# Attention scores of two tiles at once on 32-row parts of the array, and the values' product first in its slot

## What is computed

```
x = x + attn(layernorm(x))               # 16 query heads of 16, 4 key/value heads, causal
x = x + cross(layernorm(x), ctx)         # same heads; keys = values = ctx, no mask; then @ Wc.T + bc
x = x + moe(layernorm(x))                # 64 experts, top 6 of 3 of 8 groups, capacity 96, plus a shared expert

scores = q @ k.T / 4                     # 64 x 64 per sequence and head
probs  = softmax(scores)                 # causal part masked in attn
out    = probs @ v
```

## Time and profile before

| | us |
|---|---|
| runs of the kernel | 842.42, 837.95, 840.81; median 840.81 |
| profiled execution, its own time | 842.78 |
| its span, first to last instruction | 841.0 |
| TensorE matmuls busy | 676.1 (80%) |
| VectorE busy | 482.0 (57%) |
| ScalarE busy | 338.5 (40%) |
| GpSimd busy | 378.1 (45%) |
| TensorE's mean granted clock | 0.905 of full speed |

### The profile page before, as it was taken

The page is one execution under the profiler, slowest core; times in us unless marked ns, Lnnn a source line. Parts: engine busy times, 40 slices in busy tenths (PEclk is TensorE's granted clock), DMA queues, the critical chain, the costliest instruction groups (busy, mean ns, idle before and its releaser), DMA issues. The chain is left out here.

```text
span 841.0 us, 16829 instructions
## 1 busy us (share of the span) xinstructions
PE 676.1 (80%) x6353; PEld 482.3 (57%) x6353; DVE 482.0 (57%) x1086; ACT 338.5 (40%) x636; POOL 378.1 (45%) x354
## 2 busy tenths in 40 slices
PE   2699999998988788888745999799999987773083
PEld 1266666676766566665412556477887765553062
DVE  3267776677868777778445999533333332321057
ACT  2477777766767646755121332112222211110000
POOL 5122222125343423431121832847776777776454
PEclk9899999998999989999756999899999999997555
DMA  7234444665532223210018000138999988953298
GB/s 218 27 59 79 79 79 77 99 98 100 100 73 62 47 45 76 48 44 29 5 44 257 2 0 1 42 96 224 239 235 228 231 211 212 225 127 40 24 302 303
DMA packets 125376, 94.30 MB, mean 112 GB/s; under 512 B 73137, under 2 KB 109169, under 8 KB 125297
## 3 DMA queue, kind: packets, MB, share of 16 engines
q1 hardware_dynamic: 96368, 74.57, 35.1%
q0 software_dynamic: 23552, 14.21, 10.2%
q10 hardware_dynamic: 5376, 4.46, 1.7%
HBM read 60.26 MB, written 24.44 MB: 101 GB/s over the span
## 5 line engine op out<-in xcount | busy, mean ns | idle before, releaser
L1229 POOL DMA_INDIRECT sum_d<-nz,tokens x64 | 118.2, 1847 | 46.8 <-issue 14.6
L724 DVE TENSOR_REDUCE mx<-Sc 128x16 f32<-128x1024 f32 x64 | 77.9, 1217 | 37.8 <-PE Sc L401 37.5
L1056 PE MATMUL bank<-xnT,sgu_sb 128*128 128x512 f32 (+1 forms) x192 | 86.9, 601 | 11.8 <-PEq L1588 11.8
L1111 PE MATMUL bank<-xT,wgu_sb 128*88 128x96 f32 x1024 | 95.1, 246 | 0.3 <-ACT xT L1180 0.3
L1279 DVE TENSOR_TENSOR hid<-sil,bank 88x192 f32<-88x192 f32 x64 | 22.4, 350 | 118.2 <-ACT sil L1186 88.6
L1111 PEld LDWEIGHTS bank<-xT,wgu_sb 128*88 128x88 f32 x1024 | 89.4, 157 | 0.6 <-issue 0.5
L600 ACT COPY ET<-ring 128x512 f32<-128x512 f32 x128 | 69.5, 589 | 44.0 <-PE ring L413 41.8
L429 PEld LDWEIGHTS O<-vbd,ET 128*64 128x64 f32 x2048 | 69.2, 142 | 25.9 <-issue 17.3
L413 PE MATMUL ring<-ident,E 128*128 128x128 f32 x512 | 73.8, 290 | 12.5 <-ACT E L639 11.5
L728 DVE TENSOR_TENSOR E<-Sc,mx 128x1024 f32<-128x1024 f32 x64 | 78.4, 1225 | 6.9 <-DVE mx L724 0.5
L401 PE MATMUL Sc<-kbd,qT 64*64 64x256 f32 x1024 | 76.4, 404 | 6.7 <-DMA kbd<-kT 6.7
(11 more groups left out here) (149 smaller groups left out, 1144.1 us busy)
## 6 DMA issues: line engine op xcount, KB each, us to landing
wgu_sb<-in_wgu_dram SPq DMA_DIRECT2D x64, 352.0 KB
wd_sb<-in_wd_dram SPq DMA_DIRECT2D x64, 176.0 KB
sum_d<-zeros SPq DMA_DIRECT2D x16, 524.0 KB, 6.4
y<-sum_d SPq DMA_DIRECT2D x16, 512.0 KB, 8.8
kbd<-kT SPq DMA_DIRECT2D x248, 32.0 KB, 2.1
X<-in_x_dram SPq DMA_DIRECT2D x8, 512.0 KB, 6.4
rows_d<-xhT SPq DMA_DIRECT2D x8, 512.0 KB, 3.0
out_dram<-X ACTq DMA_DIRECT2D x8, 512.0 KB, 5.2
```

The lines of the kernel that those rows point to most:

```text
L724: nc.vector.reduce_max(mx[:, m % 2, :], sc, AX.X).then_inc(s_mx, 1)
L1056: last = nc.tensor.matmul(out[0:m, :], sgu[:, e, k * MS + m0:k * MS + m0 + m], xnT[:, e, TOK * g:TOK * (g + 1)], start=e == 0, stop=e == 1)
L1111: last = nc.tensor.matmul(GP[e % 2][0:MH, CAP * u:CAP * (u + 1)], wgu[:, j, 4 * MH * c + MH * u:4 * MH * c + MH * (u + 1)], xT[:, e % 2, c ...
L1229: pool.indirect_dma_start(w["sums"][e % 2], bass.IndirectOffsetOnAxis(ap=tokens[0:CAP - 1, e:e + 1], axis=0), outs[0:CAP - 1, e % EB, :], ...
```

## The change

Each product of the scores is cut in two: 32 rows (two heads) by 64 queries, with 128 columns. A pair `p` of tiles is computed in one call, into one PSUM tile `Sc` of four banks, bank `r` for the 32 rows `32r`. The mask is 512 columns wide and goes over both tiles of the pair at once. `scores(p)` waits until VectorE has subtracted both tiles of the pair before. It is called in even slots only, two tiles ahead, and comes after `pv` and `out_t`. `pv(m-1)` moves from the slot's end to its beginning. Waits that counted tiles count pairs. The order of the heads in `E` changes with the banks, and `pair_of` with it. VectorE's two instructions have the same elements in another access pattern.

```
@@ pair_of
-    r, c, m = j // 4, j // 2 % 2, j % 2
-    return 4 * c + 2 * r + m
+    r, c = j // 2, j % 2
+    return 4 * c + r
@@ block_keys (SyncE); the same change in ScalarE's xt and queries
-                    sp.wait_ge(s_sc, 4 * (g - 1))
+                    sp.wait_ge(s_sc, 2 * (g - 1))
@@ TensorE
-            def scores(m):
-                g, t = m // GT, m % GT
+            def scores(p):
+                g, t = 2 * p // GT, 2 * p % GT
                 cross = is_cross(g)
                 if t == 0:
                     pe.wait_ge(s_kbd, KDMA * (g + 1))
                     pe.wait_ge(*saved(("XT1" if cross else "Q1", g)))
-                if m >= 2:
-                    pe.wait_ge(s_sub, m - 1)
-                for c in range(2):
-                    if not cross:
-                        for r, b in ((0, 0), (1, 0), (0, 1), (1, 1)):
-                            rows = slice(64 * r, 64 * (r + 1))
-                            nc.tensor.matmul(Sc[m % 2][64 * b:64 * (b + 1), r, 256 * c:256 * (c + 1)],
-                                             ident_bf[rows, rows], mask[rows, :], start=True, stop=False)
-                    for r, b in ((0, 0), (1, 0), (0, 1), (1, 1)):
-                        rows = slice(64 * r, 64 * (r + 1))
-                        at = 128 * t + 64 * b
-                        last = nc.tensor.matmul(Sc[m % 2][64 * b:64 * (b + 1), r, 256 * c:256 * (c + 1)],
-                                                qT[rows, g % 2, c, at:at + 64],
-                                                kbd[g % 2][rows, c, 2 * t + b].rearrange("p h k -> p (h k)"),
-                                                start=cross, stop=True)
+                if p >= 1:
+                    pe.wait_ge(s_sub, 2 * p)
+                if not cross:
+                    for r in range(0, 4, 2):
+                        for k, b in ((0, 0), (1, 0), (0, 1), (1, 1)):
+                            rows = slice(64 * k, 64 * (k + 1))
+                            nc.tensor.matmul(Sc[64 * b:64 * (b + 1), r + k, :], ident_bf[rows, rows], mask[rows, :],
+                                             start=True, stop=False)
+                for n in range(2):
+                    for c in range(2):
+                        for b in range(2):
+                            at = 128 * (t + n) + 64 * b
+                            for r in range(4):
+                                rows = slice(32 * r, 32 * (r + 1))
+                                last = nc.tensor.matmul(
+                                    Sc[64 * b:64 * (b + 1), r, 256 * n + 128 * c:256 * n + 128 * (c + 1)],
+                                    qT[rows, g % 2, c, at:at + 64],
+                                    kbd[g % 2][rows, c, 2 * (t + n) + b, 2 * (r % 2):2 * (r % 2) + 2].rearrange(
+                                        "p h k -> p (h k)"), start=cross, stop=cross or (n == 1 and c == 1),
+                                    tile_position=(32 * r, 64 * b))
                 last.then_inc(s_sc, 1)
@@ TensorE's slots
             for m in range(FIRST, LAST):
-                if 0 <= m + 1 < 2 * NT:
-                    scores(m + 1)
+                if 0 <= m - 1 < 2 * NT:
+                    pv(m - 1)
                 if crossed(m - 2):
                     out_t(m - 2)
+                if m % 2 == 0 and 0 <= m + 2 < 2 * NT:
+                    scores(m // 2 + 1)
                 if 0 <= m < 2 * NT:
                     probs_t(m)
...
-                if 0 <= m - 1 < 2 * NT:
-                    pv(m - 1)
@@ VectorE's shift(m)
-                dve.wait_ge(s_sc, m + 1)
-                sc = Sc[m % 2][:].rearrange("p r (h k) -> p (r h) k", k=S)
+                dve.wait_ge(s_sc, m // 2 + 1)
+                sc = Sc[:, :, 256 * (m % 2):256 * (m % 2 + 1)].rearrange("p r (h k) -> p r h k", k=S)
@@ memory
-        mem["mask"] = sb("mask", [128, HQ * S], BF16)
+        mem["mask"] = sb("mask", [128, HH * S], BF16)
-        mem["Sc"] = [pb(f"Sc{k}", [128, 2, 512]) for k in range(2)]
+        mem["Sc"] = pb("Sc", [128, 4, 512])
```

More of the change, by code:

```diff
@@ L541, in xt @@
                     if v == 0:
-                        act.wait_ge(s_sc, 4 * (g - 1))
+                        act.wait_ge(s_sc, 2 * (g - 1))
                     nc.scalar.activation(qT[:, g % 2, :, cols].rearrange("p c (t q) -> p c t q", t=2), src,
@@ L721, in shift @@
             def shift(m):
-                dve.wait_ge(s_sc, m + 1)
-                sc = Sc[m % 2][:].rearrange("p r (h k) -> p (r h) k", k=S)
-                nc.vector.reduce_max(mx[:, m % 2, :], sc, AX.X).then_inc(s_mx, 1)
+                dve.wait_ge(s_sc, m // 2 + 1)
+                sc = Sc[:, :, 256 * (m % 2):256 * (m % 2 + 1)].rearrange("p r (h k) -> p r h k", k=S)
+                nc.vector.reduce_max(mx[:, m % 2, :].rearrange("p (r h) -> p r h", r=4), sc, AX.X).then_inc(s_mx, 1)
                 if m >= 2:
@@ L727, in shift @@
                 dve.wait_ge(s_mx, m + 1)
-                nc.vector.tensor_tensor(E_[:, m % 2, :].rearrange("p (h k) -> p h k", k=S), sc,
-                                        mx[:, m % 2, :].unsqueeze(2).to_broadcast([128, H, S]),
+                nc.vector.tensor_tensor(E_[:, m % 2, :].rearrange("p (r h k) -> p r h k", r=4, k=S), sc,
+                                        mx[:, m % 2, :].rearrange("p (r h) -> p r h", r=4).unsqueeze(3).to_broadcast(
+                                            [128, 4, 4, S]),
                                         ALU.subtract).then_inc(s_sub, 1)
@@ L1526, in _ @@
                     nc.gpsimd.affine_select(out=m, in_=m, compare_op=ALU.is_ge, fill=MASKED,
-                                            base=0, pattern=[[0, HQ], [-1, S]],
+                                            base=0, pattern=[[0, HH], [-1, S]],
                                             channel_multiplier=1).then_inc(s_const, 1)
```

## The result

The changed kernel takes 893.36 us (median of 4 runs, 888.49 to 897.22) where the kernel before, timed beside it, takes 839.45 (837.95 to 842.42): 1.0635 times as long, with a 95% interval of 1.0571 to 1.0698. The forecast was 870 with a range of 842 to 892: the sign was right and the size too small, by 23 us, just outside the range. The profiled run took 897.22 us, its span 895.5, its mean granted clock 0.878 (0.905 before).

The account below looks back on a forecast made before the run. TensorE was taken to bound self attention; in cross attention TensorE and VectorE wait for each other. Terms 5 + 10 + 1 + 7 - 6 = +17, plus 12 for the clock, gave +29: 870 us, range 842 to 892.

Parts of the forecast that it names:

- The products' length: Scores in both attentions: eight array parts at once, a cross pair 1.05 us instead of 2.1, self 1.65 instead of 2.42.
- The values' product first: `pv` at the slot's head: cross attention's wait for it goes, 4.0 us a group; self attention's start gains 1.
- The keys a slot later: Self attention: TensorE stands 1.7 us a group for key DMAs, groups take 21.35 us against 20.74; +5 in all.
- The passage: From self to cross attention: key loops of 22.4 and 24.4 us in place of 19.7 and 17.4; +10.
- Until routing: Stretch between the passage to cross attention and the start of routing: +1 us.
- The lone PSUM tile: Cross attention: VectorE stands 2.85 us each even slot, less the vanished `pv` wait; net +7 us over four groups.
- The end: Last three attention slots have no scores and `pv` comes first: -6 us (-2 to -9).
- The clock: Pauses before cross pairs' scores: some ten more falls to half clock at 1.2 us each, +12 (0 to +25).
- the keys' loop of the self groups: Self attention: scores, next key copy, then 13.2 us to landing; 21.35 us against 20.74, +0.6 six times.
- no further falls: Rival for the attentions: the clock falls no more often than before; +17, 858 us, chance 0.24.
- four parts at once: Rival for the scores' products: only four array parts work together; +20, 890 us, chance 0.14.
- hidden transfers: Rival for self attention: key DMAs stay hidden and TensorE remains the bound; 825 us, chance 0.13.

Follow-up runs that it names:

- e6: Changed kernel with the values' product moved back to the slot's end: 995.18 us, 1.1817 times the kernel before.
- e1: Kernel before with only the values' product and `out_t` moved ahead of the scores, to the slot's head: 896.25 us, 1.0667 times the kernel before.
- e8: Changed kernel with half of each group's key transfers (8 of 16) issued from GpSimd's queue instead of SyncE's: 862.85 us, 1.0264 times the kernel before.
- e4: Changed kernel with ten idle products filling TensorE's pause before the pair's scores: 871.33 us, 1.0359 times the kernel before.
- e3: Kernel before with only TensorE's wait for a group's key DMAs made one slot earlier: 873.79 us, 1.04 times the kernel before.
- e11: Changed kernel with the pair's scores called behind `wc` in all stages and key transfers in two queues: 820.43 us, 0.9683 times the kernel before.
- e13: Changed kernel with key transfers in two queues, self groups' scores at the slot's head, cross groups' behind `wc`: 802.31 us, 0.9522 times the kernel before.
- e10: Changed kernel with the pair's scores called behind `probs_t` and `wc` in the same even slot: 825.92 us, 0.9798 times the kernel before.

## Why the prediction was right in sign and wrong in size

- **The products' length**: right. 64 instructions in 1.21 us warm, the self pair 1.70 against 1.65.
- **The values' product first**: right as a gain inside the new order (`e6`), and larger than anything else in it. The prediction did not see that the gain hangs on scores being two tiles ahead; `e1` would have been forecast wrongly, and was.
- **The keys a slot later**: right in mechanism (TensorE waits for the transfers once a self group; `e8` removes the wait and the loss together), and the term that was sized worst. `e4` tells it apart: up to att(42) it has two falls, as many as before. Up to the copy of group 8 (197.19 against 182.54) it has lost 14.6 us where the prediction had 5 for all of self attention. The passage, to the copy of group 10, adds 8.1 against the forecast 10. So the passage was about right and the self groups were 10 too cheap: after needs 22.5 a group (copies from 42.14 to 199.88, in seven), not 21.35. The way from copy to scores is 13.58 (154.51 to 168.09) against 13.2, since 16 issues took 11.35 and not 10.97. The way from scores to copy is 8.11 as forecast (8.15) in the group shown, but 9.53 in the next (168.09 to 177.62), whose clock had fallen. And 3 us are lost in the very first group, with two queues too, where 1 was to be won; why is open. That waiting for the keys a slot earlier costs this much by itself `e3` shows, +29.4 by att(42) on the old order.
- **Until routing**: forecast +1. From the copy of group 10 to that of 12 `e4` loses 8.3 more and `e8` 5.7. `e11`, which differs from `e8` only in the later place of the scores, gains 5.0 on before there: the pair's scores stand in front of `wc` here as in the routed groups, and the prediction had charged that to the routed ones alone.
- **The lone PSUM tile**: the wait was right. It went from L735 to L753's successor L759, once in two slots, 2.5 to 2.9 us with the clock held up against the forecast 2.85 (whose own terms, 3.0 less 0.25, give 2.75). Of what it costs, less is known: att(42) to att(58) costs +6.0 in `e4` (34.4 - 28.4) against +7, but `e4` has two falls there and before four.
- **The end**: forecast -6. After gives back 1.1, with as much of the lower clock between att(58) and att(63) as before (10.2 us); `e4` gives 5.3 (34.4 - 29.1), but without any fall there. So this term was up to 5 too large.
- **The clock**: the pause before the pair was right (2.3 to 2.8 us forecast, 2.34 shown). The count came out, ten more falls forecast and 11 counted (19 - 8), but partly by luck: the ten were those of cross attention, and five of the 11 lie before the copy of group 8, where before has none. The price was near: 1.2 us each forecast; `e4` gives back 22.0 for 15 falls, 1.5 each. The 44.4 us more at the lower clock (81.9 - 37.5) can have cost 22.2 at most. Many falls begin at the pair's scores (400.8, 168.7), so scores and transposes lie in them, and VectorE's wait for that chain grows from 2.94 to 4.45.
- **What was never asked**: whether the pair has to be at the head of the cross slot. The prediction worked out that `probs_t` and `wc` stand behind the scores and priced it at 2.85 us a slot, but took the placement as given. It was the dearest part: 60.5 us with its clock (`e13` against `e8`).

What failed is the size of terms of the sum, above all the keys' loop of the self groups and the stretch until routing: together with the passage they were put at +16 and measured +28.4 by att(42), at an equal number of falls. In the profiled runs after is 54.5 us over before where the sum had 29. Of the 25 missing, 12 are in the attentions without the further falls (+29.1 by att(63) in `e4` against +17) and 7 more come with them (48.3 - 29.1 = 19.2 against 12). The last 6 lie behind the attentions, where they can't be told from the spread of that stretch. Since `e4` has four falls fewer than before, the first share is rather larger than 12.

The rivals: no further falls (858) is refuted by the count and by what `e4` wins; four parts at once by the 1.21 us; hidden transfers by the 2.4 us waits. `e8` shows what that last rival said, self attention faster than before if the transfers are short enough: it put the point at 11.5 us.

## What to carry to other kernels

Work computed further ahead may stand in a slot only behind what the other engine needs in that same slot; ask of each moved call what is queued behind it, and ask it for each stage, since the best place differed between the two stages (802 us with each its own, 820 with the later place in both). Two changes to an order aren't summed from single trials: the values' product first cost 56 us in one order and saved 102 in the other. And price a pause of TensorE with everything that runs in the slow stretch behind it: here some 1.5 us for each fall of the clock, beside the pause itself.

## What the runs showed of the hardware beyond that

- Products on parts of 32 rows by 64 columns ran eight at once in fp32: 64 instructions of 128 columns in 1.21 us, 0.15 us for each eight and everything around them.
- The length of a pause did not by itself tell whether the clock fell. In after, pauses of 2.39 us until 168.09 and 2.34 until 400.79 were followed by the lower level, one of 2.51 until 146.40 was not. In `e10`, of the equal pauses of 1.93 us once in each self group, two were followed by it (until 87.83 and 152.69) and four were not. The pauses of 0.95 and 0.96 us in the routed slots of `e10` and `e13` never were.
- Small transfers of 32 KB take a median of 0.61 us each to issue on SyncE and 0.53 on GpSimd (`e8`), some on SyncE twice as long, and the two queues ran side by side: 16 issues in 6.5 us in place of 11.4. The median time to land rose from 2.1 us to 3.0.
